# Two chained attention layers on one core: moving statistics, reciprocals and the final step in the order of three engines

## The reference

```python
h = group_norm(x, w, b)                  # 32 groups of 2 channels, per image
q, k, v = h @ Wq + bq, h @ Wk + bk, h @ Wv + bv
attn = softmax(q @ k.T * 64 ** -0.5)     # 1024 x 1024 per image
x = x + (attn @ v) @ Wo + bo
```

## Time and profile before

| | |
|---|---|
| time, median of 3 runs | 239.01 us (236.49 to 240.69) |
| profiled execution, time | 236.29 us |
| its span, first to last instruction | 234.3 us |
| mean granted TensorE clock | 0.932 |
| busy: TensorE, Pool, VectorE, ScalarE | 199.0, 151.0, 135.0, 101.5 us |
| instructions on them (matmuls; Pool; VectorE; ScalarE) | 1216, 93, 184, 136 |

### The profile page before, as it was taken

The page is one execution under the profiler, slowest core; times in us unless marked ns, Lnnn a source line. Parts: engine busy times, 40 slices in busy tenths (PEclk is TensorE's granted clock), DMA queues, the critical chain, the costliest instruction groups (busy, mean ns, idle before and its releaser), DMA issues.

```text
span 234.3 us, 3189 instructions
## 1 busy us (share of the span) xinstructions
PE 199.0 (85%) x1216; PEld 106.0 (45%) x1216; DVE 135.0 (58%) x184; ACT 101.5 (43%) x136; POOL 151.0 (64%) x93
## 2 busy tenths in 40 slices
PE   8868467999999499994999599986999979949980
PEld 7654334455555244543455255444545434514420
DVE  1558962657687445856388357926588639005343
ACT  3422303744657036550574338531556444434610
POOL 1200001979688944699386958697487979997905
PEclk9995757999999958998899999997999999999998
DMA  7150320140041000500014000500032100010011
GB/s 225 48 134 0 76 59 1 36 101 1 0 93 46 0 3 0 134 1 4 0 27 107 1 3 0 134 4 0 0 73 66 45 1 0 4 45 0 0 45 45
DMA packets 4718, 9.14 MB, mean 39 GB/s; under 512 B 800, under 2 KB 1760, under 8 KB 4704
## 3 DMA queue, kind: packets, MB, share of 16 engines
q1 hardware_dynamic: 4272, 8.42, 14.1%
q10 hardware_dynamic: 432, 0.53, 0.6%
HBM read 1.58 MB, written 1.05 MB: 11 GB/s over the span
## 4 chain that ended last, share of the span: by engine, by line
PE 53%; POOL 20%; issue 8%; DVE 7%; ACT 4%; POOLq 0%
PE ps_attn L614 14%; POOL prob_sum L235 12%; PE ps_max L574 6%; PE ps_scores L594 5%; DVE neg_max L426 4%; PE ps_scores L596 4%; PE ps_scores L602 4%; PE ps_scores L598 4%; PE ps_misc L564 4%; PE ps_scores L556 3%; POOL attn L241 3%; POOL xs L244 3%; ACT probs L327 3%; PE ps_misc L621 3%; DVE stats L380 1%
## 5 line engine op out<-in xcount | busy, mean ns | idle before, releaser
L235 POOL TENSOR_TENSOR prob_sum<-prob_sum,probs 128x1024 f32<-128x1024 f32 x44 | 104.3, 2371 | 22.6 <-ACT probs L327 19.0
L426 DVE TENSOR_REDUCE neg_max<-ps_max 128x1 f32<-128x1024 f32 x59 | 72.1, 1222 | 42.5 <-PE ps_max L575 42.3
L327 ACT ACTIVATE probs<-ps_scores 128x1024 f32<-128x1024 f32 x64 | 62.8, 1023 | 71.6 <-PE ps_scores L603 71.3
L614 PE MATMUL ps_attn<-probs,vals 128*64 128x512 f32 x256 | 63.8, 619 | 0.0
L574 PE MATMUL ps_max<-keys,q_hi 64*128 64x512 f32 x59 | 28.6, 485 | 16.3 <-DVE neg_max L426 16.3
L224 POOL TENSOR_TENSOR rstd<-var_eps,minus_half 128x1 f32<-128x1 f32 x8 | 4.4, 549 | 51.3 <-DVE var_eps L396 51.3
L434 DVE RECIPROCAL rden<-den 128x128 f32<-128x128 f32 x28 | 26.0, 938 | 12.7 <-ACT den L333 12.7
L614 PEld LDWEIGHTS ps_attn<-probs,vals 128*64 128x64 f32 x256 | 15.9, 138 | 29.0 <-issue 20.1
L575 PE MATMUL ps_max<-keys,q_hi 64*128 64x512 f32 x59 | 28.7, 486 | 0.0
L574 PEld LDWEIGHTS ps_max<-keys,q_hi 64*128 64x128 f32 x59 | 11.3, 192 | 36.4 <-DVE neg_max L426 21.6
L594 PE MATMUL ps_scores<-q_hi,keys 64*128 64x512 f32 x64 | 27.2, 425 | 0.0
(11 more groups left out here) (78 smaller groups left out, 310.5 us busy)
## 6 DMA issues: line engine op xcount, KB each, us to landing
keys<-keys SPq DMA_DIRECT2D x16, 256.0 KB, 3.4
q_hi<-q_hi SPq DMA_DIRECT2D x16, 128.0 KB, 2.3
xs<-x_dram SPq DMA_DIRECT2D x4, 256.0 KB, 4.3
out_dram<-xs SPq DMA_DIRECT2D x3, 256.0 KB, 2.0
layer<-layers_dram ACTq DMA_DIRECT2D x2, 194.5 KB, 4.5
q_row<-max_rows SPq DMA_DIRECT2D x16, 2.0 KB
out_dram<-xs SPq DMA_DIRECT2D x4, 64.0 KB, 1.6
const_sb<-consts_dram ACTq DMA_DIRECT2D x1, 128.0 KB, 3.6
```

The lines of the kernel that those rows point to most:

```text
L235: pool.tensor_tensor(prob_sum[u % 2][:, :], first[:, :], probs[t][:, :], ALU.add).then_inc(added, 1)
L327: act.activation(probs[t][:, :], ps_scores[t % 2][:, :], ACT.Exp, scale=SCALE).then_inc(exp_done, 1)
L426: dve.tensor_reduce(neg_max[u % 2][:, t:t + 1], ps[:, :], AX.X, ALU.max, negate=True).then_inc(max_done, 1)
L614: mm = pe.matmul(ps_attn[half * C:(half + 1) * C, :], v, probs[t][:, cols], start=(t == 0), stop=(t == TILES - 1))
```

## The change

Nothing is added or taken away; three engines get another order.

- Pool engine: the final step of unit w - 1 comes ahead of the fourth addition of unit w; before it came ahead of the sixth.
- VectorE: reciprocal 1 comes ahead of the two low parts, reciprocals 2 and 3 directly behind them and ahead of maximum 6; maxima 6 and 7 and both lead maxima follow one another, and the statistics come behind the second lead maximum.
- TensorE: the matmul of the group mean comes behind the first scores tile of the unit; before it came ahead of it.

```diff
@@ gpsimd
                 for t in range(1, TILES if w < LAST else EARLY):
-                    if t == 6 and w:
+                    if t == 4 and w:
                         finish(w - 1)
                     add(w, t)
@@ vector
                     reciprocal(w - 1, 0)
                 if nxt:
                     row_max(w + 1, 5)
+                if w:
+                    reciprocal(w - 1, 1)
                 if prep:
                     low_q(w + 2)
                     low_k(w + 2)
                 if w:
-                    reciprocal(w - 1, 1)
+                    reciprocal(w - 1, 2)
+                    reciprocal(w - 1, 3)
                 if nxt:
                     row_max(w + 1, 6)
-                if w:
-                    reciprocal(w - 1, 2)
-                if nxt:
                     row_max(w + 1, 7)
-                if w:
-                    reciprocal(w - 1, 3)
                 if prep:
                     row_max(w + 2, 0)
+                    row_max(w + 2, 1)
                 if w + 3 < UNITS:
                     if w + 3 >= B:
                         dve.wait_ge(final_done, w + 3 - B + 1)
                     gn_own(w + 3)
-                if prep:
-                    row_max(w + 2, 1)
@@ tensor
                 next_max(2)
+                scores(w, 0)
                 if prep:
                     pe.wait_ge(max_staged, w + 1)
                     group_mean_of(w + 2)
-                scores(w, 0)
```

## The result

| | before | after |
|---|---|---|
| time, median | 239.85 us (4 runs, 236.49 to 241.78) | 218.83 us (4 runs, 218.53 to 221.25) |
| profiled execution, time / span | 236.29 / 234.3 us | 218.53 / 216.3 us |
| mean granted TensorE clock | 0.932 | 0.935 |
| TensorE busy | 199.0 us (85%) | 195.1 us (90%) |

The ratio to before is 0.9227, with a 95% interval of 0.9088 to 0.9365: the kernel is faster by 6 to 9%. The forecast of 219.5 us (215 to 226) was met. The mean clock did not move, although the low stretches of units 2, 3 and 5 are gone: unit 0 ran at 0.75 for 0.87 and the last 23.7 us at 0.91 for 0.97.

A forecast was written before the change was run, and what follows sets the result against it. TensorE was taken as the bound, resting 3.1 us in four units. Gains of 14.9 (units 1 to 4), 0.9 (unit 5) and 1.6 (unit 6) took 236.29 to 218.9; 0.6 added for low clock gave 219.5 us, range 215 to 226.

The forecast's parts named there:

- TensorE bounds, and the rest at the head of four units is to be won: TensorE, busy 199.0 of 234.3 us, rests 3.1 us in each of four units; 12.4 us to gain.
- The lead maximum ahead of the statistics removes it: On VectorE, the second lead maximum, queued behind the statistics, starts earlier; this removes 3.1 us from units 1 to 4.
- 4.8 us in hand: Final step ends at 72.66 in unit 1; statistics, wanted at 77.5, have 4.8 us to spare.
- The final step fills the Pool engine's idle time: Final step fills a 1.64 us Pool hole after additions 2 and 3; loop 21.4 us against a unit of 22.38.
- A new wait of 0.56 us before maximum 7: Early reciprocals delay maximum 6, so TensorE waits 0.56 us per unit; 2.8 us cost in units 1 to 5.
- The clock: Without rests, units 2, 3 and 5 run at full clock, gaining 3.2, 1.5 and 1.45 us.
- Unit 6: TensorE's 1.63 us wait for the sum at its head goes; maximum 6's delay of about 1.2 us is hidden.
- A: Rests go but the clock still falls in some units; two units about 224 us, five up to 235; chance 0.10.
- B: Loop through the Pool engine binds; TensorE waits 0.5 to 1.5 us a unit for the sum, 222 to 228; chance 0.07.
- C: Some other wait keeps TensorE resting about 3 us per unit; 235 to 240 us; chance 0.02.
- D: Pool and VectorE instructions collide, 1.06 us each; five a unit give about 245 us, slower than before; chance 0.03.

The follow-up runs named there:

- L alone: Kernel before with only the second lead maximum moved ahead of the statistics; 226.72 us, ratio 0.945.
- P and R: Kernel before with only the final step ahead of the fourth addition and the reciprocals early; 219.06 us, ratio 0.920.
- the filled kernel: Kernel before with six extra matmuls, results unused, in each of the four TensorE rests, order untouched; 234.92 us, ratio 0.985.
- P alone: Kernel before with only the final step moved ahead of the fourth addition; 245.16 us, ratio 1.022.
- the kernel without R: Changed kernel with the reciprocals back at their old places; 244.93 us, ratio 1.023.
- R alone: Kernel before with only the reciprocals moved early; 238.88 us, ratio 0.994.
- M alone: Kernel before with only the mean's matmul moved behind the first scores tile; 244.25 us, ratio 1.018.
- all but P: Changed kernel with the final step back ahead of the sixth addition; 224.93 us, ratio 0.939.

## Why the prediction was right

- *TensorE bounds, and the rest at the head of four units is to be won.* Right: no such rest is left, 12.4 us of them.
- *The lead maximum ahead of the statistics removes it.* This step credited a part that this kernel does not need. The maximum's new place does remove the wait by itself (L alone), but beside P and R it is redundant: without it the time is the same (219.96, 0.919 against 0.923). The statistics of the changed kernel begin right behind the maximum, waiting for nothing, because the final step has ended 4.7 us ahead of them (at 72.63 + 1.27 = 73.90 in the rows of the next point):

```profile
77.46 1.23 DVE L426 TENSOR_REDUCE neg_max<-ps_max 128x1 f32<-128x1024 f32 x1 [0.88 <-PE ps_max L572]
78.60 0.68 DVE L380 BATCH_NORM_STATS2 stats<-xs 128x6 f32<-128x512 f32 x1
```

My own working had that number, 4.8 us in hand, and should have read from it that the maximum no longer needed to overtake anything. The place would matter only with a late final step, as L alone shows.
- *The final step fills the Pool engine's idle time.* Right, and the loop through it is the tightest place. It was placed at 21.4 us for a unit of 22.38; with the reciprocals at their old places the loop is 24.9 and the kernel slower than before. The Pool engine's timeline after, beside the earlier trace rows: 1.64 us idle before became 0.24 (0.6 forecast), with the final step in the gap.

```profile
66.14 4.88 POOL L235 TENSOR_TENSOR prob_sum<-prob_sum,probs 128x1024 f32<-128x1024 f32 x2 [0.90 <-ACT probs L327]
71.26 1.29 POOL L241 TENSOR_TENSOR attn<-attn,rden 128x512 f32<-128x512 f32 x1 [0.24 <-DVE rden L434]
72.63 1.27 POOL L244 TENSOR_TENSOR xs<-attn,xs 128x512 f32<-128x512 f32 x1
73.86 9.93 POOL L235 TENSOR_TENSOR prob_sum<-prob_sum,probs 128x1024 f32<-128x1024 f32 x4
```

- *A new wait of 0.56 us before maximum 7.* Mis-sized: the units are 21.9 us, not 22.38, so it is 0.1 us at most and 2.4 us of cost did not come in five units. VectorE's timeline, beside the earlier trace rows, shows where the 0.5 us went:

```profile
67.34 0.94 DVE L434 RECIPROCAL rden<-den 128x128 f32<-128x128 f32 x1
68.20 0.65 DVE L412 SCALAR_TENSOR_TENSOR q_lo<-ps_scores,bias_q,q_hi 128x512 fp32r<-128x512 f32 x1
68.77 0.74 DVE L419 SCALAR_TENSOR_TENSOR keys<-ps_scores,bias_k,keys 128x512 fp32r<-128x512 f32 x1
69.43 1.75 DVE L434 RECIPROCAL rden<-den 128x128 f32<-128x128 f32 x2
71.10 1.16 DVE L426 TENSOR_REDUCE neg_max<-ps_max 128x1 f32<-128x1024 f32 x1
```

Here an instruction whose input is there starts before the end of the one ahead: two reciprocals take 1.75 us, not 1.88; the low part starts 0.86 after the start of the reciprocal and not 0.94; the maximum starts 1.67 after the start of the pair. I had laid whole durations end to end.
- *The clock.* Right for units 1 to 5, and shown by the filled kernel, not only argued. What I missed is that unit 0's low stretch has a length that differs from one kernel to the next by about 2 us with nothing in the program changed up to there; here it took back 1.8 us, in a stretch that the working called untouched. It and the 2.4 us of the new wait cancelled, which is why a working with two errors of 2 us came out within 1 us. The parts of the mechanism are measured, but that closeness of the total is luck.
- *Unit 6.* 1.6 us forecast, 1.3 found: with shorter units TensorE arrives earlier, so it waits 0.26 us for the sum. The wait of about 1.2 us before maximum 7 there was 0.74, covered by the Pool engine's chain as said: the wait for the sum in unit 7 is 2.16 us for 3.15, and the stretch is 21.06 us long as before.
- *The rivals.* A, that the low clock stays in units 1 to 5, did not happen. (Its case for units 1 and 4, "with TensorE never idle", misreads: they hold 3.1 us of idle time at their end.) B did not in this kernel, but is what P alone and the kernel without R are: the loop binds, and TensorE waits 2.4 to 3.3 us a unit for the sum. C, another wait that keeps the rests, did not happen either. D, a collision of Pool and VectorE: additions 2 and 3 took 4.88 us with three reciprocals beside them (67.34, and the pair at 69.43), as long as before with one, so no. The kernels that came out slower with the early final step did so by the loop and not by such a collision.

## What to carry to other kernels

When a chain runs in a loop over several engines, move the step and what feeds it together: here the final step's earlier place cost 2% alone and, with its reciprocals early, gained 8%. Ask of each part of a change what it would bring without the others; the part that takes away the wait in the trace need not be the one that is needed. And where TensorE's rests bring a lower clock behind them, price a rest by what follows it too: 12.4 us of rests stood for some 16 to 17.

## What the runs showed of the hardware

The granted clock fell to 0.50 behind 10 of the 12 rests of about 3 us ahead of a unit in the traces of before (3 of 4, in the earlier trace rows not behind the third), R alone (3 of 4) and M alone (4 of 4). It fell behind some shorter waits too: with P alone behind two of the four waits of 2.4 to 2.75 us for the sum, in all but P behind the 2.18 us in unit 7, where the changed kernel kept 1.00 behind 2.16, and with L alone behind one of four rests of 1.67 us, the one in unit 4:

```profile
101.33:124.79 23.46, 21.79 (x140) 11.31 (x138) 16.42 (x22) 12.34 (x16) 19.64 (x11) 1.00 0.15 35
124.79:149.77 24.98, 23.31 (x140) 12.20 (x138) 16.42 (x22) 12.43 (x16) 19.59 (x11) 0.93 0.14 33
```

What decides between such cases these runs do not show. Unit 0, which starts at the low clock, had one of two lengths with the same instructions ahead of it. So two executions can differ by 2 us with no cause found in the program, and an effect of that size is read from waits and unit lengths and not from the total.
